# The last piece of x issued as two transfers, 120 partitions and then 8, in a convolution kernel

## The chip, the cores and the metric

The kernel runs on one core of one Trainium2 chip. The metric is device microseconds of an execution, the median of several runs. A core has TensorE (matmuls; PE in the profile, PEld for its weight loads), VectorE (DVE), ScalarE (ACT), GpSimd (POOL) and SyncE (SP), each with an instruction stream of its own. The engines wait for each other on semaphores. Data comes from memory by transfers (DMAs) that an engine issues; 16 DMA engines carry them out.

## The reference

x has the shape (4, 1024, 48, 48). It is normalised over 32 groups of channels per image, and then a recurrence runs down the 48 rows and back up. Each step multiplies the row before with a 1024 x 1024 matrix, adds a bias, takes the positive part and adds the row:

```python
def _gn(v, G=32, eps=1e-05):
    g = v.reshape(B_, G, C_ // G, H_, W_)
    m = mean(g, axis=(2, 3, 4)); s = var(g, axis=(2, 3, 4))
    return ((g - m) / sqrt(s + eps)).reshape(v.shape)
def step(carry, x):                     # Wm: the middle tap of W, 1024 x 1024
    new = relu(einsum('oc,ncw->now', Wm, carry) + bb) + x
    return (new, new)
_, ys = scan(step, xs[0], xs[1:])                       # down, rows 1 to 47
down = concatenate([xs[:1], ys])
_, ys2 = scan(step, down[-1], down[:-1], reverse=True)  # up, rows 46 to 0
return x + concatenate([ys2, down[-1:]])
```

Nothing of the recurrence can begin before the mean and the variance of all of x are known.

## The kernel before

Channels are split into K = 8 blocks of P = 128 partitions. The 48 rows are split into six groups of eight rows; x lies in memory as one block of 128 x 12288 floats for each group. In the first stage SyncE loads the groups one after another, alternately into two buffers (x_ring and d_rows), and each in pieces of a few channel blocks, as LOADS (line 33) lists them. The group loaded last (index LAST = 5, which is also the group that stays in x_ring for the first rows of the recurrence) has five pieces: blocks 0-1, 2-3, 4-5, 6 and 7. The fifth piece is channel block 7: 128 partitions with 6144 bytes each, 768 KB. load_group (line 260) issues one transfer for a piece, at line 267, after waits that say that the buffer's blocks have been read by VectorE (line 264) and ScalarE (line 265). Each piece has a semaphore of its own, stat_loaded[g][n], which a transfer raises by 16 when it has landed.

The order of SyncE's work is written out by hand: groups 0 to 4, then eight tiles of the weights (line 278, t from 0 to 7), then group 5 (line 280), then the other eight tiles (line 281), 256 KB each. After that SyncE waits until the first row is normalised (line 284) and goes on to the stores and loads of the recurrence.

The statistics are shared between two engines. VectorE takes bn_stats of each image of a channel block (line 476, channel_stats), and ScalarE does the same with two accumulating activations for two blocks of a group (lines 394 and 399, block_moments); ACT_BLOCKS (line 36) gives it blocks 3 and 7 of the first groups and blocks 1 and 5 of the last. For the last group VectorE goes piece by piece (lines 505 to 509): it waits for the piece, takes its statistics, and aggregates (line 501, channel_moments) the blocks that LAST_MOMENTS (line 37) lists for that piece: none for the first, then blocks 0 and 1, 2 and 3, 4, and 6, 5 and 7 after the fifth. When all eight blocks have moments, TensorE averages them over the groups of 32 channels (line 602), VectorE makes the spread, TensorE averages again (line 605), ScalarE takes the root (line 415), and VectorE normalises the first row (lines 535 and 538). ScalarE rounds the weight tiles (line 379, w_round) in between: tiles 8 to 11 after its last statistics and before the root, tiles 12 to 15 after it. GpSimd makes the rounding remainder of each tile (line 318), ten of them before it waits for the first row.

Then the recurrence runs on TensorE, in 283 jobs of 24 matmuls each in three-term split precision (lines 627, 634 and 640), with the other engines moving and splitting the products.

Of the kernel before, what the change touches and what calls it, by code (L numbers as in the profile page):

```python
# [12 lines left out]
P = 128  # L13
# [16 lines left out]
RING = 8  # L30
GROUPS = H // RING
LAST = GROUPS - 1
LOADS = (((0, 2), (2, 4), (4, 8)),) + (((0, 4), (4, 8)),) * (LAST - 1) + (((0, 2), (2, 4), (4, 6), (6, 7), (7, 8)),)
EARLY = RING * COLS // NI * LAST
WARM = 8
ACT_BLOCKS = ((3, 7),) * LAST + ((1, 5),)
LAST_MOMENTS = ((), (0, 1), (2, 3), (4,), (6, 5, 7))
# [33 lines left out]
def second_done(i):  # L71
    return 2 * i + 2
# [7 lines left out]
def build(nc, x_groups, w_t, bias, down_rows, out_groups):  # L80
    with ExitStack() as ctx:
# [3 lines left out]
        def sem(name):  # L85
            return ctx.enter_context(nc.semaphore(name))
# [28 lines left out]
        channels = [turn[:, (1 + t) * HALF:(2 + t) * HALF].rearrange("p (k c) -> p k c", k=KB) for t in range(2)]  # L115
        bn = turn[:, 0:K * NI * LAST * BN_DIM].rearrange("p (c s) -> p c s", c=K * NI)
        bn_late = turn[:, K * NI * LAST * BN_DIM:K * NI * (LAST * BN_DIM + BN_DIM + 3)].rearrange("p (c s) -> p c s", c=K * NI)

        def act_stat(g, k):

            images = slice(k * NI, (k + 1) * NI)
            return bn[:, images, 3 * g:3 * g + 3] if g < LAST else bn_late[:, images, 3:6]

        def act_count(g, k1):

            return sum(len(ks) for ks in ACT_BLOCKS[:g]) + sum(k < k1 for k in ACT_BLOCKS[g])

        def w_place(t):

            o, n = divmod(t, K)  # L130
            return o, KB * blocks_of(o)[n // KB] + n % KB
# [11 lines left out]
        def landing(g):  # L143

            return x_ring if g % 2 == 0 or g == LAST else d_landing

        def stats_count(g, k1):

            return sum(len(p) for p in LOADS[:g]) + [b for _, b in LOADS[g]].index(k1) + 1

        def stats_free(g, k1):

            older = g - 1 if g == LAST else g - 2
            return stats_count(older, min(b for _, b in LOADS[older] if b >= k1))

        def stat_cols(ring, i):
            return ring[:, i // NI, :, i % NI * WIDTH:(i % NI + 1) * WIDTH]

        def spare(n):

            return xn[:, n, 0:RING * WIDTH].rearrange("p (r w) -> p r w", r=RING)
# [5 lines left out]
        def row_in(groups, h, k0=0, k1=K):  # L167

            return groups[h // RING].rearrange("p (k r e) -> p k r e", k=K, r=RING)[:, k0:k1, h % RING, :]

        def ring_row(h, k0=0, k1=K):
            return x_ring[:, k0:k1, h % RING, :]
# [41 lines left out]

        stat_loaded = [[sem(f"stat_loaded{g}_{n}") for n in range(len(LOADS[g]))] for g in range(GROUPS)]
        bias_loaded = sem("bias_loaded")
# [40 lines left out]
        @block.sync  # L257
        def _(sp):

            def load_group(g):  # L260
                ring = landing(g)
                for n, (k0, k1) in enumerate(LOADS[g]):
                    if g >= 2:
                        sp.wait_ge(stats_done, stats_free(g, k1))
                        sp.wait_ge(act_read, act_count(g - 1 if g == LAST else g - 2, k1))
                    there = x_groups[LAST - g].rearrange("p (k e) -> p k e", k=K)[:, k0:k1, :]
                    sp.dma_start(ring[:, k0:k1, :, :].rearrange("p k r e -> p k (r e)"), there
                                 ).then_inc(stat_loaded[g][n], 16)

            def load_weights(t):  # L270
                o, k = w_place(t)
                sp.dma_start(w_raw[t], w_t[k, :, o * HALF:(o + 1) * HALF]).then_inc(w_loaded[t], 16)

            for g in range(LAST):
                load_group(g)
            sp.wait_ge(stats_done, stats_count(LAST - 2, K))
            sp.wait_ge(act_read, act_count(LAST - 2, K))
            for t in range(W_FRONT):
                load_weights(t)
            load_group(LAST)  # L280
            for t in range(W_FRONT, W_TILES):
                load_weights(t)

            sp.wait_ge(first_row, 4)
            sp.dma_start(down_rows[0, :, :], d_ring[:, 0, :]).then_inc(d_stored[0], 16)
            sp.dma_start(ring_row(0), row_in(x_groups, RING)).then_inc(x_loaded[0], 16)

            for h in range(1, H - RING):
                sp.wait_ge(y_ready, second_done(CHUNKS * h - 1))
                sp.dma_start(down_rows[h, :, :], d_ring[:, h % RING, :]).then_inc(d_stored[h % RING], 16)  # L290
                sp.dma_start(ring_row(h), row_in(x_groups, h + RING)).then_inc(x_loaded[h % RING], 16)

            for h in reversed(range(1, H)):
                sp.wait_ge(out_ready, CHUNKS * (H - h))
                sp.dma_start(row_in(out_groups, h), ring_row(h)).then_inc(out_stored[h % RING], 16)
                if h >= RING:
                    sp.wait_ge(d_stored[h % RING], 16 * LAST)
                    sp.dma_start(d_ring[:, h % RING, :], down_rows[h - RING, :, :]).then_inc(d_loaded[h % RING], 16)
                above = h + 1
                if RING <= above < H:  # L300
                    sp.wait_ge(out_stored[above % RING], 16 * ((H - 1 - above) // RING + 1))
                    sp.dma_start(ring_row(above), row_in(x_groups, above - RING)
                                 ).then_inc(x_loaded[above % RING], 16)
            sp.wait_ge(out_ready, CHUNKS * H)
            sp.dma_start(row_in(out_groups, 0, KB, K), ring_row(0, KB, K)).then_inc(out_stored[0], 16)
            for n, (k0, k1) in enumerate(LAST_PIECES):
                sp.wait_ge(last_out, n + 1)
                sp.dma_start(row_in(out_groups, 0, k0, k1), ring_row(0, k0, k1)).then_inc(out_stored[0], 16)
            for r in range(RING):
                sp.wait_ge(out_stored[r], 16 * (GROUPS if r else GROUPS + len(LAST_PIECES)))  # L310
# [62 lines left out]
        def _(act):  # L373
# [14 lines left out]
            def block_moments(g, k):  # L388
                count = act_count(g, k + 1)
                piece = [k < b for _, b in LOADS[g]].index(True)  # L390
                neg = act_neg[:, g, ACT_BLOCKS[g].index(k), :]
                act.wait_ge(stat_loaded[g][piece], 16)
                for n in range(NI):
                    final = act.activation(spare(n), stat_cols(landing(g), k * NI + n), ACT.Identity,  # L394
                                           scale=-1.0 / (RING * WIDTH), accum_out=neg[:, n:n + 1])
                final.then_inc(act_summed, 1)
                act.wait_ge(act_summed, count)
                for n in range(NI):
                    final = act.activation(spare(n), stat_cols(landing(g), k * NI + n), ACT.Square,  # L399
                                           bias=neg[:, n:n + 1], accum_out=act_stat(g, k)[:, n, 2:3])  # L400
                final.then_inc(act_read, 1)
                act.activation(act_stat(g, k)[:, :, 1], neg, ACT.Copy, scale=-1.0).then_inc(act_means, 1)
                act.wait_ge(act_read, count)
# [56 lines left out]
        def _(dve):  # L460
# [9 lines left out]
            def channel_stats(g, k0, k1):  # L470
                ring = landing(g)
                for i in range(k0 * NI, k1 * NI):
                    if i // NI in ACT_BLOCKS[g]:
                        continue
                    out = bn[:, i, g * BN_DIM:(g + 1) * BN_DIM] if g < LAST else bn_late[:, i, 0:BN_DIM]
                    final = dve.bn_stats(out, stat_cols(ring, i))  # L476
                return final

            for g in range(LAST):
                for n, (k0, k1) in enumerate(LOADS[g]):  # L480
                    dve.wait_ge(stat_loaded[g][n], 16)
                    channel_stats(g, k0, k1).then_inc(stats_done, 1)

            dve.memset(bn_late[:, :, BN_DIM:BN_DIM + 1], float(EARLY))
# [18 lines left out]

            dve.wait_ge(early_ready, 2)
            for n, (k0, k1) in enumerate(LOADS[LAST]):
                dve.wait_ge(stat_loaded[LAST][n], 16)
                channel_stats(LAST, k0, k1).then_inc(stats_done, 1)
                dve.wait_ge(stats_done, stats_count(LAST, k1))
                channel_moments(LAST_MOMENTS[n])
# [183 lines left out]
```

## Time and profile before

| what | value |
|---|---|
| time, median of 3 runs | 1658.34 us (1658.21 to 1658.56) |
| span of the profiled execution | 1656.3 us |
| its mean granted clock of TensorE | 1.000 of full speed |
| TensorE matmul busy | 1546.1 us (93% of the span) |
| ScalarE busy | 1358.5 us (82%) |
| VectorE busy | 1141.4 us (69%) |
| GpSimd busy | 960.0 us (58%) |
| first averaging matmul of the moments | at 102.56 us |
| first matmul of the recurrence | at 107.75 us |

The span runs from the first to the last instruction of one profiled execution; the profile gives no other time for that execution, and what lies before and after the span (launch and end) is in the runs' times alone. The chain of waits is followed back from the last instruction: at each step to what released it, or to the instruction before it on its engine. In a timeline, what stands in square brackets behind a row is idle time of the engine before it, and what ended it. A transfer's time to landing runs from its issue until its semaphore is complete.

### The profile page before, as it was taken

The page shows a single profiled execution, that of the slowest core. Times are in us where ns is not written, and L with a number is a line of the kernel's source. Part 1 is how long each engine was busy: PE and PEld are TensorE (multiplying, and loading weights), DVE is VectorE, ACT ScalarE, POOL GpSimd, SP SyncE. Part 2 cuts the span into 40 slices and gives each one's busy share as a digit, 9 for nine tenths or more (in the row PEclk, how much of TensorE's full clock was granted, in tenths as well). Part 3 has the DMA queues.
Part 4 walks back from the last instruction along what each step waited for, and adds up shares of the span by engine and source line. Part 5 has one row for each costly group of instructions (what it writes and reads, how often), then busy time and mean ns, then how long its engine had stood idle before and what let it go on. Part 6 is the DMA issues. An engine that isn't in the chain of part 4 may idle for free.

```text
span 1656.3 us, 23710 instructions
## 1 busy us (share of the span) xinstructions
PE 1546.1 (93%) x6812; PEld 1277.0 (77%) x6812; DVE 1141.4 (69%) x3355; ACT 1358.5 (82%) x4265; POOL 960.0 (58%) x1096
## 2 busy tenths in 40 slices
PE   0049999999999999999999999999999999999998
PEld 0037888888888888888888888888888888888886
DVE  5786666766766667666676666766766667666676
ACT  5658888888888888888888888888888888888887
POOL 0066766767667666676675555555555555555554
PEclk9999999999999999999999999999999999999999
DMA  9952323232323232231001444444453535454211
GB/s 406 422 224 77 106 86 115 77 115 77 115 77 115 88 104 96 96 104 50 1 1 54 157 132 155 149 137 152 135 168 119 171 122 166 125 162 135 95 58 58
DMA packets 149555, 207.06 MB, mean 125 GB/s; under 512 B 4016, under 2 KB 135088, under 8 KB 147632
## 3 DMA queue, kind: packets, MB, share of 16 engines
q1 hardware_dynamic: 149280, 205.54, 37.1%
q8 instruction: 54, 0.88, 0.2%
q14 instruction: 77, 0.63, 0.1%
q10 hardware_dynamic: 144, 0.00, 0.0%
HBM read 136.32 MB, written 69.21 MB: 124 GB/s over the span
## 4 chain that ended last, share of the span: by engine, by line
PE 91%; DMA 4%; DVE 3%; ACT 1%; issue 0%; POOL 0%; SPq 0%; ACTq 0%; DVEq 0%
PE bank L640 30%; PE bank L634 30%; PE bank L627 30%; DMA x_ring<-x_groups 4%; DVE turn L476 1%; DVE turn L562 0%; ACT turn L439 0%; DVE d_rows L538 0%; DVE d_rows L535 0%; ACT turn L430 0%; DVE st_lo L542 0%; DVE d_rows L577 0%; DVE moments L501 0%; ACT xn L399 0%; DVE turn L557 0%
## 5 line engine op out<-in xcount | busy, mean ns | idle before, releaser
L627 PE MATMUL bank<-w_hi,st_hi 128*128 128x512 f32 (+1 forms) x2264 | 881.4, 389 | 0.0
L640 PE MATMUL bank<-w_hi,st_lo 128*128 128x512 f32 (+1 forms) x2264 | 880.0, 389 | 0.6 <-DVE st_lo L542 0.3
L634 PE MATMUL bank<-w_lo,st_hi 128*128 128x512 f32 (+1 forms) x2264 | 879.9, 389 | 0.0
L355 POOL TENSOR_TENSOR st_lo<-d_rows,st_hi 128x256 fp32r<-128x256 f32 x650 | 464.0, 738 | 578.0 <-ACT st_hi L448 578.0
L430 ACT ACTIVATE turn<-turn 32x128 f32<-32x128 f32 x2256 | 697.0, 309 | 65.6 <-DVE turn L557 41.6
L562 DVE STREAM_TRANSPOSE turn<-bank 32x128 f32<-32x128 f32 x2256 | 709.6, 315 | 35.5
L640 PEld LDWEIGHTS bank<-w_hi,st_lo 128*128 128x128 f32 (+1 forms) x2264 | 424.2, 187 | 90.8 <-POOL st_lo L355 1.2
L627 PEld LDWEIGHTS bank<-w_hi,st_hi 128*128 128x128 f32 (+1 forms) x2264 | 424.4, 187 | 89.3 <-ACT st_hi L448 0.4
L634 PEld LDWEIGHTS bank<-w_lo,st_hi 128*128 128x128 f32 (+1 forms) x2264 | 424.4, 187 | 89.1 <-issue 0.2
L439 ACT ACTIVATE turn<-turn,bias_sb 128x128 f32<-128x128 f32 (+1 forms) x1132 | 362.4, 391 | 41.8 <-DVE turn L562 3.5
L448 ACT ACTIVATE st_hi<-d_rows 128x256 fp32r<-128x256 f32 x650 | 237.3, 414 | 137.9 <-DVE d_rows L577 137.9
L577 DVE TENSOR_TENSOR d_rows<-turn,xn 128x256 f32<-128x256 f32 x282 | 107.8, 423 | 199.9 <-ACT turn L439 199.9
L577 DVE TENSOR_TENSOR d_rows<-turn,d_rows 128x256 f32<-128x256 f32 x281 | 106.9, 422 | 197.5 <-ACT turn L439 197.5
L349 POOL TENSOR_TENSOR x_ring<-x_ring,d_rows 128x512 f32<-128x512 f32 x143 | 184.8, 1293 | 7.2 <-DVE d_rows L577 7.2
L557 DVE STREAM_TRANSPOSE turn<-bank 128x256 f32<-128x256 f32 (+1 forms) x283 | 127.3, 450 | 48.2 <-PE bank L640 47.6
L336 POOL TENSOR_TENSOR xn<-xn,gn_rstd 128x512 f32<-128x512 f32 x141 | 150.1, 1065 | 11.1
L334 POOL TENSOR_TENSOR xn<-x_ring,gn_mean 128x512 f32<-128x512 f32 x141 | 150.4, 1066 | 0.0
L602 PE MATMUL bank<-moments,group_avg 128*128 128x32 f32 x2 | 0.6, 396 | 102.6 <-DVE moments L501 102.6
L602 PEld LDWEIGHTS bank<-moments,group_avg 128*128 128x128 f32 x2 | 0.5, 309 | 102.5 <-issue 102.5
L318 POOL TENSOR_TENSOR w_lo<-d_rows,w_hi 128x512 fp32r<-128x512 f32 x16 | 21.9, 1398 | 95.1 <-ACT w_hi L379 89.7
L476 DVE BATCH_NORM_STATS2 turn<-x_ring 128x6 f32<-128x384 f32 x96 | 45.2, 544 | 18.2 <-DMA x_ring<-x_groups 18.1
L394 ACT ACTIVATE xn<-x_ring 128x384 f32<-128x384 f32 x32 | 16.3, 511 | 24.0 <-DMA x_ring<-x_groups 24.0
(45 smaller groups left out, 125.5 us busy)
## 6 DMA issues: line engine op xcount, KB each, us to landing
x_ring<-x_groups SPq DMA_DIRECT2D x82, 768.0 KB, 7.2
out_groups<-x_ring SPq DMA_DIRECT2D x47, 768.0 KB, 5.1
down_rows<-d_rows SPq DMA_DIRECT2D x40, 768.0 KB, 3.8
d_rows<-down_rows SPq DMA_DIRECT2D x40, 768.0 KB, 6.6
x_ring<-x_groups SPq DMA_DIRECT2D x5, 3072.0 KB, 23.6
d_rows<-x_groups SPq DMA_DIRECT2D x4, 3072.0 KB, 23.9
x_ring<-x_groups SPq DMA_DIRECT2D x5, 1536.0 KB, 10.9
d_rows<-w_t SPq DMA_DIRECT2D x16, 256.0 KB, 11.9
```

Of the source, the lines that this page charges most:

```text
L334: pool.tensor_tensor(dst, x_chunk(h, c), table(gn_mean), ALU.subtract).then_inc(centred, 1)
L336: pool.tensor_tensor(dst, dst, table(gn_rstd), ALU.mult).then_inc(xn_ready, 1)
L349: pool.tensor_tensor(x_chunk(h, c), x_chunk(h, c), by_image(d_chunk(h, c)), ALU.add).then_inc(out_ready, 1)
L355: final = pool.tensor_tensor(slot(st_lo, at, b * KB, (b + 1) * KB), d_chunk(row_of(i), i % CHUNKS, b * KB, (b + 1) * KB), slot(st_hi, at, ...
L430: final = act.activation(target(j, q, u), source(blocks, q, u), ACT.Copy)
L439: final = act.activation(cols, cols, ACT.Relu, bias=bias_sb[:, k:k + 1])
L448: final = act.activation(slot(st_hi, at, b * KB, (b + 1) * KB), d_chunk(row_of(i), i % CHUNKS, b * KB, (b + 1) * KB), ACT.Copy)
L562: final = dve.transpose(target(j, q, u), source(bank[j % BANKS], q, u))
L577: dve.tensor_tensor(here, product_of(j, i), addend, ALU.add).then_inc(y_ready, 1)
L627: return pe.matmul(bank[j % BANKS][0:used(j), :], stationary(st_hi, j, k), w_cols(w_hi, o, k), start=(n == 0), stop=False)
L634: return pe.matmul(bank[j % BANKS][0:used(j), :], stationary(st_hi, j, k), w_cols(w_lo, o, k), start=False, stop=final)
L640: return pe.matmul(bank[j % BANKS][0:used(j), :], stationary(st_lo, j, k), w_cols(w_hi, o, k), start=False, stop=final)
```

## The change

The fifth piece of the last group is issued as two transfers, partitions 0 to 119 and then partitions 120 to 127. Both raise the same semaphore by 16, and VectorE waits for 32 on it. All other pieces are issued as before, and all waits for them ask for 16.

```diff
+UNEVEN = 120
...
+        def parts(g, n):
+
+            return ((0, UNEVEN), (UNEVEN, P)) if (g, n) == (LAST, len(LOADS[LAST]) - 1) else ((0, P),)
+
+        def piece_landed(g, n):
+            return 16 * len(parts(g, n))
...
                     there = x_groups[LAST - g].rearrange("p (k e) -> p k e", k=K)[:, k0:k1, :]
-                    sp.dma_start(ring[:, k0:k1, :, :].rearrange("p k r e -> p k (r e)"), there
-                                 ).then_inc(stat_loaded[g][n], 16)
+                    here = ring[:, k0:k1, :, :].rearrange("p k r e -> p k (r e)")
+                    for p0, p1 in parts(g, n):
+                        sp.dma_start(here[p0:p1], there[p0:p1]).then_inc(stat_loaded[g][n], 16)
...
             for n, (k0, k1) in enumerate(LOADS[LAST]):
-                dve.wait_ge(stat_loaded[LAST][n], 16)
+                dve.wait_ge(stat_loaded[LAST][n], piece_landed(LAST, n))
                 channel_stats(LAST, k0, k1).then_inc(stats_done, 1)
```

The same replacement of 16 by piece_landed(g, n) stands in block_moments (ScalarE) and in the loop over the first five groups (VectorE), where it gives 16.

## Rows read from the trace of the kernel before

**Rows 1.** The page's part 4: shares of the chain by engine, by line.
```profile
PE 91%; DMA 4%; DVE 3%; ACT 1%; issue 0%; POOL 0%; SPq 0%; ACTq 0%; DVEq 0%
PE bank L640 30%; PE bank L634 30%; PE bank L627 30%; DMA x_ring<-x_groups 4%; DVE turn L476 1%; DVE turn L562 0%; ACT turn L439 0%; DVE d_rows L538 0%; DVE d_rows L535 0%; ACT turn L430 0%; DVE st_lo L542 0%; DVE d_rows L577 0%; DVE moments L501 0%; ACT xn L399 0%; DVE turn L557 0%
```

**Rows 2.** Chain in order of time, 75.5 to 108 us: start, us, what.
```profile
76.06 14.21 DMA x_ring<-x_groups
...
102.56 0.62 PE bank L602 x2
...
104.57 0.30 ACT gn_std L415
...
107.73 0.43 ACT st_hi L383
```

**Rows 3.** Timeline of SyncE's issues, 82 to 119 us: start, us, what.
```profile
82.94 0.33 SPq L267 DMA_DIRECT2D x_ring<-x_groups  x1
83.36 0.39 SPq L267 DMA_DIRECT2D x_ring<-x_groups  x1
83.84 0.39 SPq L267 DMA_DIRECT2D x_ring<-x_groups  x1
84.28 0.43 SPq L272 DMA_DIRECT2D d_rows<-w_t  x1
...
91.14 1.70 SPq L272 DMA_DIRECT2D d_rows<-w_t  x1
118.01 0.33 SPq L285 DMA_DIRECT2D down_rows<-d_rows  x1
```

**Rows 4.** DMA issues, one window each: pieces 3, 4, 5, tiles 8, 15, bias.
```profile
x_ring<-x_groups SPq DMA_DIRECT2D x1, 1536.0 KB, 11.0
x_ring<-x_groups SPq DMA_DIRECT2D x1, 768.0 KB, 13.2
x_ring<-x_groups SPq DMA_DIRECT2D x1, 768.0 KB, 14.7
d_rows<-w_t SPq DMA_DIRECT2D x1, 256.0 KB, 14.9
d_rows<-w_t SPq DMA_DIRECT2D x1, 256.0 KB, 12.6
...
bias_sb<-bias ACTq DMA_DIRECT2D x1, 4.0 KB, 4.3
```

**Rows 5.** Timeline of VectorE, 90 to 103 us.
```profile
90.37 3.78 DVE L476 BATCH_NORM_STATS2 turn<-x_ring 128x6 f32<-128x384 f32 x8 [0.63 <-DMA x_ring<-x_groups]
...
97.29 1.90 DVE L476 BATCH_NORM_STATS2 turn<-x_ring 128x6 f32<-128x384 f32 x4
99.22 0.40 DVE L501 BATCH_NORM_AGGREGATE moments<-turn 128x2 f32<-128x9 f32 x4
99.54 1.90 DVE L476 BATCH_NORM_STATS2 turn<-x_ring 128x6 f32<-128x384 f32 x4
101.47 0.94 DVE L501 BATCH_NORM_AGGREGATE moments<-turn 128x2 f32<-128x9 f32 x12
```

**Rows 6.** Issues by line: ns least, median, most; all 12, last 8.
```profile
L267 SPq DMA_DIRECT2D x_ring<-x_groups x12: 327/352/438, 0.7 to 83.8; - x12
...
L272 SPq DMA_DIRECT2D d_rows<-w_t x8: 424/435/2952, 84.3 to 91.1; - x8
```

**Rows 7.** DMA queue 94.5 to 95.5 (packets, MB, share); windows, DMA share last but one.
```profile
q1 hardware_dynamic: 68, 0.41, 101.7%
...
101.50:102.00 0.50, 0.00 (x0) 0.00 (x0) 0.50 (x8) 0.37 (x1) 0.50 (x1) 1.00 0.24 90
...
102.50:103.00 0.50, 0.44 (x2) 0.47 (x2) 0.00 (x0) 0.00 (x0) 0.00 (x0) 1.00 0.08 29
```

**Rows 8.** Timeline of ScalarE, 99 to 105 us.
```profile
99.27 2.60 ACT L379 ACTIVATE w_hi<-d_rows 128x512 fp32r<-128x512 f32 x4 [0.45 <-DMA d_rows<-w_t]
104.57 0.29 ACT L415 ACTIVATE gn_std<-bank,eps 128x32 f32<-128x32 f32 x1 [2.70 <-PE bank L605]
```

**Rows 9.** Timeline of GpSimd, 96 to 118 us.
```profile
107.78 9.65 POOL L318 TENSOR_TENSOR w_lo<-d_rows,w_hi 128x512 fp32r<-128x512 f32 x6 [5.30 <-DVE d_rows L538]
```

More of the change, by code:

```diff
@@ L391, in block_moments @@
                 neg = act_neg[:, g, ACT_BLOCKS[g].index(k), :]
-                act.wait_ge(stat_loaded[g][piece], 16)
+                act.wait_ge(stat_loaded[g][piece], piece_landed(g, piece))
                 for n in range(NI):
@@ L480, in _ @@
                 for n, (k0, k1) in enumerate(LOADS[g]):
-                    dve.wait_ge(stat_loaded[g][n], 16)
+                    dve.wait_ge(stat_loaded[g][n], piece_landed(g, n))
                     channel_stats(g, k0, k1).then_inc(stats_done, 1)
```

## The prediction

> **What bounds the kernel now.** I read the chain of waits first, by engine and line [rows 1]: TensorE holds 91% of the 1656.3 us span, and the three matmul lines of the main loop take 30% each. Loading x (L267) has 4%. So the body after about 108 us is matmuls in a fixed order, and a change to one load of x can only shift the moment at which they begin: one us later there is one us at the end, and nothing in the body gives it back or enlarges it.
>
> Then I read the same chain in order of time between 75 and 108 us [rows 2]. The last DMA on it is the second of the five pieces of group 5: issued at 76.06, landed 14.21 later, at 90.28. The next transfer on this chain would have to be the piece that the change splits, and it is not there: from 90.37 on the chain is VectorE, until TensorE averages the moments at 102.56, ScalarE takes the root at 104.57, and the split of the first row follows at 107.73.
>
> The changed piece is the fifth. SyncE issues pieces 3, 4 and 5 at 82.94, 83.36 and 83.84, and weight tile 8 at 84.28 [rows 3]. The table of DMA issues gives 11.0, 13.2, 14.7 and 14.9 us from issue to landing [rows 4]. Their landings are thus 93.94, 96.56, 98.54 and 99.18 us. The last weight tile, issued at 91.14, lands 12.6 later, at 103.7.
>
> VectorE's timeline [rows 5] tells when the fifth piece is wanted. After a wait of 0.63 us ending at 90.37, no row carries a wait: statistics of one piece and aggregation of the blocks before it alternate without a gap. The fourth piece's statistics start at 97.29, an aggregation at 99.22, and the fifth piece's statistics at 99.54. The piece landed at 98.54, so it lies **1.0 us** before its use. ScalarE reads blocks 1 and 5 of this group, which are in pieces 1 and 3; it does not read the fifth.
>
> **The change, part by part.**
>
> *One more DMA issue on SyncE.* An issue from L267 takes 0.33 to 0.44 us, median 0.35; the eight weight issues behind it take 0.42 to 2.95 [rows 6]. Nearest is the issue at 83.84 itself, 0.39; the extra one may cost 0.35 to 2.95, since I have no row for a shorter partition count. It moves eight issues and nothing else: tile 8 goes from 84.28 to about 84.7, at worst 87.2, and it lands at 99.18 behind x, so more than 11 us of queue cover it. After the eight issues SyncE waits for the first row until 118.01 [rows 3]; its spare time there is 118.01 - (91.14 + 1.70) = 25 us. ScalarE's and GpSimd's queues hold no DMA in this stretch. Value taken: 0. Without that cover the cost would be the whole 0.4 us on tile 8.
>
> *The same bytes, otherwise divided.* Price of one row of 6144 B: in the stretch from 94.5 to 95.5, x alone moves, with 68 packets and 101.7% of 16 engines [rows 7]: 16 x 1.017 us / 68 = 0.239 us a packet, and 0.41 MB / 68 is 6.0 KB, one row. With 128 rows over 16 engines, 8 a piece, a piece costs 1.9 us, against 2.0 between the landings of pieces 4 and 5. In the likeliest division the 120 rows still go eight to an engine, on all engines but one, and the 8 rows add one row to some. Those engines end 0.24 us later, and with completion packets no more than one further packet later: landing at 98.8 to 99.0, 0.5 to 0.7 us before use. The excluded ends: all 120 rows on one engine is 112 rows more than its eight, 112 x 0.239 = 26.8 us; an engine relieved of its eight rows may finish 1.9 us earlier. Value taken: +0.24 on the landing, 0 on the end, because the row price and the 16 busy engines of [rows 7] are the nearest rows.
>
> One rule of the Trainium skill bears on the division. The page "DMA: Bandwidth & Descriptors", section "Why a DMA increments its semaphore by 16 and not by 1", says that a DMA issued from SyncE uses the largest number of engines, up to 16, that divides its partition count. That would make 15 engines for 120 rows and 8 for 8 rows, hence nine rows on eight engines, eight on seven, none on the last. By it the sum is +0.24 on the landing and 0 on the end, and rival A below has no place; by the trace alone the engine count is open.
>
> *A price of the second transfer itself.* The low end is weight tile 8: 256 KB that land 0.64 us behind piece 5, or 410 GB/s, the pace of x, so nothing is paid for being a transfer of its own in a filled queue. The high end is the 4 KB bias load at the start of the kernel, 4.3 us from issue to landing [rows 4]. Value: 0, since tile 8 stands directly behind the changed piece in the same queue, while the bias load went out from ScalarE as the first of x was issued, and its 4.3 us were not hidden behind transfers ahead of it.
>
> A rule that speaks against the change: the same page, section "Anatomy of one DMA — SWDGE (gpsimd) path", counts a fixed 2.0 us for each transfer, and its section "Rules for kernel authors" says that one under 64 KB pays mostly overhead; the second part has 48 KB. By it the landing would be at 100.5 and the end at 1659.3; by tile 8's row, 0. The 2.0 us are given for DMAs that GpSimd issues, and the trace has none.
>
> *A late engine.* The share of busy DMA engines falls to 0.24 between 101.5 and 102 and is still 0.08 between 102.5 and 103 [rows 7], that is 3.8 and then 1.3 of 16 engines, while the last tile lands only at 103.7. So one engine or two end about 2 us behind the rest, and a landing is that of the latest. If it is the late engine that loses its rows, the fifth piece lands up to 1.9 us earlier, at 96.6; if it gains one, 0.24 later. Either way VectorE starts on it at 99.54: it is busy with piece 4. Value: 0.
>
> *The wait on VectorE* asks for 32 in place of 16, once. Behind it in VectorE's order are four statistics (99.54, 1.90 us) and twelve aggregations (101.47, 0.94 us) [rows 5], for which TensorE waits; this is the place where lateness would bite. Its check is one instruction as before: 0.
>
> *Weights behind it.* Tile 8 already makes ScalarE wait 0.45 us before the four roundings at 99.27, which end at 101.87; ScalarE then waits 2.70 us for TensorE before the root [rows 8]. A tile 0.24 later uses up 0.24 of those 2.70. GpSimd takes its remaining six weight tiles only at 107.78, released by VectorE [rows 9]. Cost 0; past 2.70 us of lateness the root and all after it would slip, and eight rows on one engine, 8 x 0.239 = 1.9 us, don't reach that.
>
> **Sum.** 0.4 us of issue under 11 us of queue, +0.24 us of landing under 1.0 us of slack, nothing elsewhere: span 1656.3 + 0.0. The median of the runs, 1658.34, lies 2.0 us above this span, and the change touches nothing there. Forecast **1658.3 us**.
>
> **Rivals.**
>
> *A: the transfer falls on few engines (slower).* Place: the fifth piece's landing, before VectorE's statistics at 99.54. Each further row on the fullest engine costs 0.239 us; it decides once over 1.0 us is added, from five further rows on. On eight engines for both parts it is 16 rows, eight more: 1.9 - 1.0 = +0.9, 1659.2 us. On five or fewer it is at least 24 + 2 rows, 18 more: 4.3 - 1.0 = +3.3, 1661.6; on a single engine 120 more rows, 28.7 - 1.0 = +27.7, 1686 us. For it: no row shows a transfer of other than 128 partitions. Against: every stretch of x in this trace keeps all 16 engines busy. The counts by the rule quoted above leave no engine with more than nine rows.
>
> *B: the small part pays its latency in the open (slower).* If its price were the bias load's 4.3 us after the first part's landing at 98.54, VectorE would wait until 102.8: +3.3, 1661.6; a price under 1.0 shows nothing. For it: 48 KB is nearer to 4 KB in size than to the 768 KB of the piece. Against: tile 8 and the queue, issued 14 us ahead, in which the small part's start lies beside the large part's rows.
>
> *C: the late engine is relieved and it shows (faster).* Only where an execution has the fifth piece later than 99.54, against this trace; then the gain is the overshoot, at most 1.9 - 1.0 = 0.9 us: 1657.4. Against: the 1.0 us slack, and VectorE without a wait since 90.37.
>
> **How the numbers follow.** Forecast 0.86; A 0.06, of which 0.03 with over 3.3 us; B 0.03, of which 0.01 with its whole price; C 0.04; 0.01 for what none of them names. The shown runs lie within 1658.21 to 1658.56, so the range 1657.4 to 1659.4 holds the forecast with this spread, C whole and A's eight-engine case; left out are the far parts of A and B. About 0.2%, 3.3 us, is what a measurement tells from no change: slower by more has 0.03 of A and 0.01 of B, faster by more the 0.01 without a case, the rest 0.95.
>
> **What would show it.** Right: two x transfers where the fifth piece was, landing at 96.6 to 99.5; VectorE still without a wait between 90.4 and 102.4; TensorE's averaging at 102.5. The engine division shows in the busy share between 97 and 104. Wrong: a DMA named before VectorE's statistics near 99.6 (A, with a busy share that stays low until the landing; B, with one that has gone on to the weights), or the fifth piece's statistics starting before 99.5 (C).

## The result and the profile after

The changed kernel takes 1660.37 us (1660.16 to 1660.68, 21 runs) against 1658.24 us for the kernel before (1658.11 to 1658.56, 21 runs): **2.13 us slower**, ratio 1.0013, interval 1.0007 to 1.0019. That is under the 0.2% that counted as a change here, but clear of the spread of the runs, and above the forecast range of 1657.4 to 1659.4. The profiled execution has a span of 1658.5 us, 2.2 more than before.

The chain of waits of the changed kernel in order of time (start, us, what) holds a DMA where before it held VectorE alone [rows 2, 5]:

```profile
84.49 17.15 DMA x_ring<-x_groups
101.67 1.95 DVE turn L485 x4
103.64 0.95 DVE moments L510 x12
```

The DMA is the fifth piece, landed at 84.49 + 17.15 = 101.64 in place of 98.54. VectorE's timeline, in the form of [rows 5]:

```profile
90.61 3.78 DVE L485 BATCH_NORM_STATS2 turn<-x_ring 128x6 f32<-128x384 f32 x8 [0.73 <-DMA x_ring<-x_groups]
...
97.89 1.94 DVE L485 BATCH_NORM_STATS2 turn<-x_ring 128x6 f32<-128x384 f32 x4 [0.27 <-DMA x_ring<-x_groups]
99.86 0.40 DVE L510 BATCH_NORM_AGGREGATE moments<-turn 128x2 f32<-128x9 f32 x4
101.67 1.94 DVE L485 BATCH_NORM_STATS2 turn<-x_ring 128x6 f32<-128x384 f32 x4 [1.40 <-DMA x_ring<-x_groups]
103.64 0.94 DVE L510 BATCH_NORM_AGGREGATE moments<-turn 128x2 f32<-128x9 f32 x12
```

The fifth piece's statistics begin at 101.67 in place of 99.54: 2.13 us, the whole of the difference. The matmul that averages the moments moves from 102.56 to 104.73, the first matmul of the recurrence from 107.75 to 109.93, and nothing after it makes up for it.

The fourth piece, which the change leaves as it was, is late too and makes VectorE wait 0.27 us. It takes 14.4 us to landing in place of 13.2 [rows 4]:

```profile
x_ring<-x_groups SPq DMA_DIRECT2D x1, 768.0 KB, 14.4
```

In the runs below it takes 14.3 to 14.7 us wherever the fifth piece alone is split by partitions, and 13.3 or 13.4 wherever no piece of x is (the split by columns among them). So the division of the transfer behind it is what slows it.

Why the piece is late stands in the windows (stretch, length, busy us of PE, PEld, DVE, ACT and POOL with the number of instructions, TensorE's granted clock, busy share of 16 DMA engines, GB/s). The changed kernel:

```profile
94.50:98.50 4.00, 0.00 (x0) 0.00 (x0) 3.69 (x22) 3.97 (x15) 0.00 (x0) 1.00 1.03 210
98.50:101.50 3.00, 0.00 (x0) 0.00 (x0) 1.73 (x7) 0.55 (x3) 0.00 (x0) 1.00 1.02 295
94.50:95.50 1.00, 0.00 (x0) 0.00 (x0) 1.00 (x10) 1.00 (x5) 0.00 (x0) 1.00 1.06 236
```

The kernel before, in the stretch of [rows 7] that gave the price of a row:

```profile
94.50:95.50 1.00, 0.00 (x0) 0.00 (x0) 1.00 (x8) 1.00 (x6) 0.00 (x0) 1.00 1.02 406
```

Together the 16 engines are as busy as before, and they move little more than half as much. Share x 16 engines x 6144 B / rate gives what a row of 6144 B costs an engine: 1.02 x 16 x 6144 / 406 = 247 ns before, 1.06 x 16 x 6144 / 236 = **442 ns** after. Some packets of the stretch after are rows of 2048 B from the weight tiles, so the 442 ns are a price of 6144 B over both sorts; a run without the tiles, below, gives 433. So engines did not fall idle; each packet took longer.

The small packets that complete a transfer tell how many engines it used: the page of before counts 4016 packets under 512 B, the page after 4023.

```profile
DMA packets 149562, 207.06 MB, mean 125 GB/s; under 512 B 4023, under 2 KB 135095, under 8 KB 147639
```

Seven more fits 15 + 8 in place of 16: 15 engines for the 120 rows and eight for the 8 rows. The rule on the page "DMA: Bandwidth & Descriptors" of the Trainium skill, section "Why a DMA increments its semaphore by 16 and not by 1", has it so. The kernels below agree: 64 + 64 partitions have 4032 such packets (16 + 16), 126 + 2 have 4016 (14 + 2).

### The profile page after: what moved, and what is told of

It is laid out like the page before. It is cut to its first block, busy times and chain, and to the rows that moved or that the text cites. A ratio compares the mean times of both kernels' runs of the same rounds, so it can differ in the third digit from the quotient of the medians.

```text
span 1658.5 us, 23711 instructions
## 1 busy us (share of the span) xinstructions
PE 1545.9 (93%) x6812; PEld 1276.8 (77%) x6812; DVE 1141.8 (69%) x3355; ACT 1358.3 (82%) x4265; POOL 960.6 (58%) x1096
## 4 chain that ended last, share of the span: by engine, by line
PE 91%; DMA 5%; DVE 3%; ACT 1%; issue 0%; SPq 0%; POOL 0%; ACTq 0%; DVEq 0%
PE bank L649 30%; PE bank L636 30%; PE bank L643 30%; DMA x_ring<-x_groups 5%; DVE turn L485 1%; DVE turn L571 0%; ACT turn L448 0%; DVE d_rows L547 0%; DVE d_rows L544 0%; ACT turn L439 0%; DVE st_lo L551 0%; DVE d_rows L586 0%; DVE turn L566 0%; SPq L277 0%; ACT st_hi L457 0%
```

## The experiments

The theory after the result: when a transfer has other than 128 partitions, its rows are handed to the engines so that several engines at a time write to the same part of the on-chip memory, and wait for each other (theory 1, collision). Rivals: partition counts that leave engines idle or are no power of two are slow as such (theory 2); a second transfer has a price of its own (theory 3). The pace of a transfer is the time that one engine takes for one row. Times with a sign are against the kernel before.

**Two halves of 64 partitions.**

```diff
-UNEVEN = 120
+UNEVEN = 64
```

> The fifth piece as partitions 0 to 63 and then 64 to 127. Theory 1 (collision: the rows of a part are handed to the DMA engines in runs of consecutive partitions, so that two engines at a time write to the same part of the on-chip memory and each packet takes about twice its 0.24 us): packets of 6144 B at about 0.45 us while the piece moves, the piece some 1.7 us later than in the kernel before, VectorE waits about 0.7 us for it, time +0.7 us. Theory 2 (partition counts that leave engines idle or are no power of two are slow): both parts use all 16 engines, packets at 0.24 us, no wait, time as before. Theory 3 (the second transfer has a price of its own of 2 to 3 us, whatever its shape): VectorE waits 1.4 us, time +2.1 us as in the changed kernel.

Measured: 1659.88 us, +1.6 us, ratio 1.0010 (1.0001 to 1.0019). A window and a row of VectorE's timeline of this kernel:

```profile
95.00:97.00 2.00, 0.00 (x0) 0.00 (x0) 1.97 (x8) 1.97 (x9) 0.00 (x0) 1.00 1.02 221
```

```profile
100.98 1.94 DVE L485 BATCH_NORM_STATS2 turn<-x_ring 128x6 f32<-128x384 f32 x4 [0.95 <-DMA x_ring<-x_groups]
```

1.02 x 16 x 6144 / 221 = 454 ns a row. Theory 2 falls: two equal halves, powers of two, on all engines, are as slow for each row. Theory 1 had the pace right (about 0.45 us) and the time too low (+0.7).

**126 and 2 partitions** (UNEVEN = 126).

> The fifth piece as partitions 0 to 125 and then 126 to 127. Theory 1 (collision): 14 engines with nine consecutive rows each, whose starts are nine apart and so seldom meet on the same part of the memory; packets at about 0.24 us, the piece about 0.7 us later than before (ten rows on the fullest engine in place of eight), inside the 1.0 us of slack, time as before. Theory 2 (idle engines, no power of two): fewer engines than 120 uses, so at least as slow as the changed kernel, +2 us or more. Theory 3 (price of a second transfer): +2.1 us.

Measured: 1660.00 us, +1.7 us, ratio 1.0011 (1.0002 to 1.0020); VectorE waits 1.54 us, until 101.72.

```profile
95.00:97.00 2.00, 0.00 (x0) 0.00 (x0) 2.00 (x8) 1.97 (x8) 0.00 (x0) 1.00 1.04 245
```

417 ns for 6144 B, over rows of x and of the weight tiles together. Theory 1, as I had stated it (time as before), missed here; theories 2 and 3 came nearer. The series and the runs with the tiles held back, below, say by what.

**A split by columns.**

Against the changed kernel; the fifth piece is split into floats 0 to 1439 and 1440 to 1535 of each row:

```diff
-            return ((0, UNEVEN), (UNEVEN, P)) if (g, n) == (LAST, len(LOADS[LAST]) - 1) else ((0, P),)
+            e = RING * COLS
+            return ((0, e * 15 // 16), (e * 15 // 16, e)) if (g, n) == (LAST, len(LOADS[LAST]) - 1) else ((0, e),)
...
-                    for p0, p1 in parts(g, n):
-                        sp.dma_start(here[p0:p1], there[p0:p1]).then_inc(stat_loaded[g][n], 16)
+                    for e0, e1 in parts(g, n):
+                        sp.dma_start(here[:, :, e0:e1], there[:, :, e0:e1]).then_inc(stat_loaded[g][n], 16)
```

> The fifth piece as two transfers of all 128 partitions, the first 1440 floats of each row and then the last 96: the same 15 to 1 split in bytes, but no change in partitions. Theory 1 (collision) and theory 2 (partition counts): packets at the pace of before, the landing at most 0.3 us later, no wait of VectorE, time as before. Theory 3 (price of a second transfer): VectorE waits for the piece, time +2.1 us.

Measured: 1658.31 us against 1658.29, ratio 1.0000 (0.9991 to 1.0009). Window and VectorE's timeline:

```profile
95.00:97.00 2.00, 0.00 (x0) 0.00 (x0) 1.97 (x7) 1.97 (x8) 0.00 (x0) 1.00 0.99 387
```

```profile
99.48 0.40 DVE L511 BATCH_NORM_AGGREGATE moments<-turn 128x2 f32<-128x9 f32 x4
99.80 1.90 DVE L486 BATCH_NORM_STATS2 turn<-x_ring 128x6 f32<-128x384 f32 x4
```

No wait, and the rate of before (388 GB/s in the same stretch). The same bytes, the same second issue, the same wait for 32: theory 3 falls, and with it everything in the change but the partitions.

**Single transfers.** Twelve transfers in the idle stretch at the turn of the recurrence, each waited for.

```diff
+            for n, (p0, p1) in enumerate(ALONE):
+                sp.dma_start(alone[p0:p1, :], x_groups[0, p0:p1, 0:LONG]).then_inc(alone_done, 16)
+                sp.wait_ge(alone_done, 16 * (n + 1))
```

> The kernel before, with twelve transfers added one at a time in the idle stretch of the DMA queues at the turn from down to up (rows of 3840 B): loads of partitions 0-127, 0-119, 120-127, 0-63, 0-111, 0-125, 0-15, 0-127, then stores of 0-127 and 0-119, then copies from memory to memory of 128 and 120 rows. The time of the whole doesn't matter. A 3840 B packet should take 0.15 us by the pace of before. Theory 1 (collision): loads of 120 and 64 partitions take about twice as long for a packet as that of 128, 112 and 126 little more than 128, 8 and 16 partitions about four times; memory to memory 120 takes as long for a packet as 128, since nothing is written on the chip. Theory 2 (partition counts): 64, 112 and 16 at the pace of 128; 120 and 126 slow, memory to memory too. Theory 3 (price of a second transfer): all packets at the same pace.

Measured, in windows that begin in the middle of the load of 120 partitions and of the last load of 128 and reach past their ends:

```profile
766.80:769.30 2.50, 2.50 (x13) 2.07 (x12) 1.16 (x3) 1.88 (x6) 1.58 (x3) 1.00 0.36 117
785.30:787.50 2.20, 2.20 (x11) 1.83 (x10) 2.10 (x7) 1.93 (x7) 2.20 (x3) 1.00 0.38 150
```

Share x 16 x 3840 B / rate: 189 ns against 156. No factor of two, and over the whole transfers none either: 0.22 us a packet for 120 partitions, 0.20 for 64, 0.22 for 16, against 0.20 for 128, where theory 1 had twice as much for 120 and 64 and four times for 16. So theory 1 missed here. In a lone transfer of at most eight rows an engine the first packets, slow for every count, weigh heavily; I took that for the reason and repeated the experiment with more to do. (The packet times in the next expectation are such means over whole transfers.)

**Series of five.**

```diff
+            for kind, rows, times in SERIES:
+                for n in range(times):
+                    here = target[rows, n * row:(n + 1) * row]
+                    memory = x_groups[0, rows, n * row:(n + 1) * row]
...
+                    sp.dma_start(into, out).then_inc(series_done, 16)
+                landed += times
+                sp.wait_ge(series_done, 16 * landed)
```

> The kernel before, with twelve series of five transfers each ahead of the first load of x, rows of 6144 B, the five issued back to back and waited for before the next series: loads of partitions 0-127, 0-119, 0-125, 0-63, 0-111, 0-15, 0-31, 0-127 again, stores of 0-127 and 0-119, copies from memory to memory of 128 and 120 rows. The whole gets some 150 us longer, which doesn't matter. Single transfers took 0.22 us a packet for 120 partitions and 0.20 for 128 when loaded, 0.23 against 0.15 when stored; a series shows the pace without the start. Theory 1 (two engines at a time write the same part of the on-chip memory): 128 at 0.24 us a packet, loads of 120, 64 and 32 at 0.4 to 0.5, 16 at 0.8 to 0.9, 126 and 112 at 0.25 to 0.35, store of 120 above store of 128, copies of 120 like copies of 128. Theory 1b (the engines meet in the main memory they read): copies of 120 slow as well. Theory 4 (it takes transfers of both divisions side by side, the piece's and its neighbours'): loads of 120 and 64 in a series of their own keep 0.24.

The windows inside the twelve series, in the order of the expectation:

```profile
5.00:11.00 6.00, 0.00 (x0) 0.00 (x0) 0.00 (x0) 0.00 (x0) 0.00 (x0) 1.00 1.02 425
17.00:29.00 12.00, 0.00 (x0) 0.00 (x0) 0.00 (x0) 0.00 (x0) 0.00 (x0) 1.00 0.95 230
35.00:43.00 8.00, 0.00 (x0) 0.00 (x0) 0.00 (x0) 0.00 (x0) 0.00 (x0) 1.00 0.89 319
50.00:56.00 6.00, 0.00 (x0) 0.00 (x0) 0.00 (x0) 0.00 (x0) 0.00 (x0) 1.00 0.98 203
61.00:71.00 10.00, 0.00 (x0) 0.00 (x0) 0.00 (x0) 0.00 (x0) 0.00 (x0) 1.00 1.01 268
74.00:76.50 2.50, 0.00 (x0) 0.00 (x0) 0.00 (x0) 0.00 (x0) 0.00 (x0) 1.00 0.93 118
81.50:84.00 2.50, 0.00 (x0) 0.00 (x0) 0.00 (x0) 0.00 (x0) 0.00 (x0) 1.00 0.75 167
89.00:95.00 6.00, 0.00 (x0) 0.00 (x0) 0.00 (x0) 0.00 (x0) 0.00 (x0) 1.00 1.02 426
101.00:107.00 6.00, 0.00 (x0) 0.00 (x0) 0.00 (x0) 0.00 (x0) 0.00 (x0) 1.00 1.02 419
112.00:119.00 7.00, 0.00 (x0) 0.00 (x0) 0.00 (x0) 0.00 (x0) 0.00 (x0) 1.00 0.93 384
126.00:132.00 6.00, 0.00 (x0) 0.00 (x0) 0.00 (x0) 0.00 (x0) 0.00 (x0) 1.00 1.00 348
140.00:146.00 6.00, 0.00 (x0) 0.00 (x0) 0.00 (x0) 0.00 (x0) 0.00 (x0) 1.00 0.95 350
```

Worked out as above, ns an engine for a row of 6144 B:

| transfer | 128 | 120 | 126 | 64 | 112 | 16 | 32 | 128 again |
|---|---|---|---|---|---|---|---|---|
| load | 236 | 406 | 274 | 475 | 370 | 775 | 441 | 235 |
| store | 239 | 238 | | | | | | |
| memory to memory | 282 | 267 | | | | | | |

In a queue of transfers, only loads depend on the partitions. From memory to memory 120 rows cost no more than 128 do, so the reads are not it (theory 1b falls), and no neighbour of another shape is needed (theory 4 falls). The slow thing is writing into the on-chip memory. Idle engines are not it either: 126 partitions leave some idle (share 0.89, about 14 of 16) and cost less than 112, which leave none (1.01).

Of what theory 1 expected, loads of 120, 64, 32 and 126 came out; 112 came out above it, 16 a little below. It missed on the stores: it had stores of 120 above those of 128, as the single transfers had shown them, and in the series they are equal.

A rule that I had not drawn on fits these steps. The page "SBUF — State Buffer" of the Trainium skill, section "Door 1: The DMA port swizzle", says that the bandwidth of a DMA depends on how many of 16 ports its partitions reach, and that bits 2 to 4 and bit 6 of the partition number choose the port. If each engine gets a run of consecutive partitions, 64 and 32 partitions put two engines on a port, and 16 put four. From 236 ns that would be 472 and 944, an estimate by that page; measured were 475, 441 and 775. With 120, engines four apart in runs of eight share ports two by two. That section makes no difference between loads and stores; the stores of 120 partitions here (238 against 239 ns) show no such loss.

The section "The descriptor swizzle" of the page "DMA: Bandwidth & Descriptors" of the Trainium skill has a transfer of 128 partitions give each engine a port of its own, and the 236 ns, the lowest of the loads, agree. Which engine got which row no run here shows. That the price depends on the partitions of a load is shown; that engines meet on a port is a reading that fits the factors.

**The change doubled** (the fourth piece split as well).

```diff
-            return ((0, UNEVEN), (UNEVEN, P)) if (g, n) == (LAST, len(LOADS[LAST]) - 1) else ((0, P),)
+            return ((0, UNEVEN), (UNEVEN, P)) if g == LAST and n >= len(LOADS[LAST]) - 2 else ((0, P),)
```

> The change doubled: the fourth piece of the last group is split into 120 and 8 partitions as well. Theory 1: each split piece takes about 3 us longer. The fourth lands 2.5 to 3 us late and VectorE waits some 2 us for it; the fifth lands about 6 us later than in the kernel before, at 104 to 105 where VectorE wanted it at 99.5, so the time is 4.5 to 5.5 us above before, 2.5 to 3.5 above the changed kernel, with the slack of 1.0 us used only once. Theory 4 (only a boundary between the two divisions costs): the fourth and fifth have the same division, so about as much as in the changed kernel, +2 us.

Measured: 1662.32 us (1661.99 to 1663.20), +4.0 us, ratio 1.0025 (1.0015 to 1.0035). The profiled execution was the longest of these, with a span of 1661.4 us, 5.1 above before. VectorE's timeline:

```profile
100.70 1.94 DVE L485 BATCH_NORM_STATS2 turn<-x_ring 128x6 f32<-128x384 f32 x4 [2.37 <-DMA x_ring<-x_groups]
102.67 0.40 DVE L510 BATCH_NORM_AGGREGATE moments<-turn 128x2 f32<-128x9 f32 x4
104.53 1.94 DVE L485 BATCH_NORM_STATS2 turn<-x_ring 128x6 f32<-128x384 f32 x4 [1.45 <-DMA x_ring<-x_groups]
```

The waits are where theory 1 put them: 2.37 us for the fourth piece and 104.53 for the start of the fifth, in this execution. But the fourth piece landed 4.1 us later than before (100.67 against 96.56), not 2.5 to 3, and the median of the runs is half a microsecond under the range. Theory 4 (+2 us) falls again. The slack is paid only once.

**The split on a weight tile.**

```diff
+                for p0, p1 in ((0, UNEVEN), (UNEVEN, P)) if t == W_FRONT else ((0, P),):
+                    sp.dma_start(w_raw[t][p0:p1], w_t[k, p0:p1, o * HALF:(o + 1) * HALF]).then_inc(w_loaded[t], 16)
```

> The kernel before, with x as it was and the split 120 and 8 put on weight tile 8, the transfer right behind the fifth piece. The packets slow down there as well and the tile lands 0.5 to 1.5 us later; ScalarE waits that much longer before its four roundings but has 2.70 us before the root, so the time is as before (within 0.3 us). If lateness of transfers cost time without a consumer in wait, by the engines or the queue, it would be +0.5 to +1.5 us. If the fifth piece, which still moves on late engines beside the tile, is slowed by the tile's packets, its landing comes nearer to 99.5 or passes it by a few tenths.

Measured: 1658.44 us, ratio 1.0001 (0.9992 to 1.0010). ScalarE's timeline:

```profile
100.51 2.26 ACT L381 ACTIVATE w_hi<-d_rows 128x512 fp32r<-128x512 f32 x4 [1.56 <-DMA d_rows<-w_t]
104.71 0.29 ACT L417 ACTIVATE gn_std<-bank,eps 128x32 f32<-128x32 f32 x1 [1.94 <-PE bank L607]
```

The tile makes ScalarE wait 1.56 us in place of 0.45 [rows 8], and its wait before the root shrinks to 1.94: lateness that ends inside a consumer's slack costs nothing. The fifth piece, here of 128 partitions again, was issued at 83.92 and took 15.4 us, so it landed at 99.3 in place of 98.54, just before VectorE wanted it at 99.68: a split transfer slows the whole one ahead of it.

**The tiles held back.** Three kernels, with 128, 126 + 2 and 120 + 8 partitions, in which SyncE waits for the fifth piece before it issues the tiles; its first issue of a tile thus marks the landing. (With 128 partitions the kernel is that of before, and the wait asks for 16.)

```diff
             load_group(LAST)
+            sp.wait_ge(stat_loaded[LAST][-1], 32)
```

> The kernel before, with the eight weight tiles behind x issued only when the fifth piece has landed. It is the control for the two runs beside it: the fifth piece lands at about 98.5 or somewhat earlier if the tiles behind it cost it anything; the tiles come 4 us or more later, and ScalarE's roundings may then delay the root.

> 126 and 2 partitions, the weight tiles held back until the piece has landed. In the kernel with 126 and 2 the piece landed at about 101.6, 3.1 us later than before, where its pace of packets (0.29 us by nine or ten rows) explains some 1.0. If the rest comes from the weight tiles that the engines without rows begin meanwhile, and whose writes meet those of the piece, it lands at 98.8 to 99.8 here, and VectorE hardly waits. If it comes from the piece's own division (the engine with ten rows is the late one, or the two rows meet each other), it lands at 101 to 102 as before.

> 120 and 8 partitions, the weight tiles held back until the piece has landed. The packets of the 120 rows still take 0.41 to 0.44 us and eight of them in a row 3.4 us in place of 1.9; the eight rows of the second part, on two of the memory's sixteen parts, up to 0.9 more. If the tiles have no share in the delay the piece lands at 101 to 101.7 as in the changed kernel; if they have, at 100 to 101.

SyncE's timeline of the three, in that order:

```profile
98.43 2.23 SPq L272 DMA_DIRECT2D d_rows<-w_t  x5
```

```profile
100.20 0.36 SPq L281 DMA_DIRECT2D d_rows<-w_t  x1
```

```profile
100.40 0.36 SPq L281 DMA_DIRECT2D d_rows<-w_t  x1
```

With 128 partitions the tiles hardly slowed the piece: it lands at 98.54 with them and at 98.43 without. With 120 + 8, 1.9 of the 3.1 us of delay are the piece's own (100.40 - 98.54), and 1.2 (101.64 - 100.40) come from the tiles; engines that have no more rows of x can begin those while others still write the piece. The queue between 95.5 and 96.5 (packets, MB, busy share), first with 120 + 8, then with 126 + 2:

```profile
q1 hardware_dynamic: 33, 0.20, 89.3%
q1 hardware_dynamic: 51, 0.31, 85.9%
```

There are no tile rows in these: 0.893 x 16 / 33 = 0.433 us a row with 120, and 0.859 x 16 / 51 = 0.270 with 126, the pace of its series. With the tiles beside it, 6144 B had cost 0.417 in the kernel with 126 + 2, and the piece landed 1.5 us later (101.7). Which of the two sorts of packets slowed the figure does not tell, but that is what theory 1 left out with 126: a transfer is slowed not only by its own division, but by a neighbour of another one too.

The landing at 100.2 is still later than the 98.8 to 99.8 that I expected. In the run with 128 partitions the busy share falls from 0.21 to 0.06, and the piece is complete at 98.43:

```profile
96.00:97.00 1.00, 0.00 (x0) 0.00 (x0) 0.97 (x6) 0.97 (x5) 0.00 (x0) 1.00 0.21 86
97.00:98.00 1.00, 0.00 (x0) 0.00 (x0) 1.00 (x8) 1.00 (x4) 0.00 (x0) 1.00 0.06 25
```

One engine or two are some 2 us behind, as the prediction had it. Whether that late engine is one of those with ten rows, which would make up the rest, was not tried. (The times of these three, 1659.26, 1661.24 and 1661.18 us in single runs for 128, 120 and 126, include ScalarE's roundings, which come after the late tiles and delay the root.)

## Why the prediction was wrong, point by point

The step that failed is "*The same bytes, otherwise divided*": its price of a row, 0.239 us, was read in a stretch where all transfers had 128 partitions, and taken over to transfers of 120 and 8. In the changed kernel 6144 B cost 0.442 us, with the tiles held back a row cost 0.433, in a series of 120 partitions 0.406. Nine rows at 0.433 are 3.9 us, in place of 1.9 for eight at 0.239; the held run has the piece 1.9 us late. A term that the sum put at nothing makes the rest: the tiles behind the piece delayed it by 1.2 us more. Where +0.24 us was forecast for the landing, +3.1 came.

- *What bounds the kernel, the slack and the translation into time* were right: the piece lay 1.0 us before its use, so 3.1 us of lateness became 2.1, and 2.13 were measured; one us at the start was one us at the end.
- *One more issue*, *the wait for 32* and *the price of the second transfer* cost nothing, as the split by columns shows, which has all three (1658.31 against 1658.29 us). The fixed 2.0 us weighed there would have put the end at 1659.3; the columns say 0. That this sum came nearer to the result than mine is chance.
- *The division* was as expected, 15 and 8 completions, from which nine rows at most on an engine follow. What I did not ask is where the rows of an engine go. I treated an engine's time for a row as its own; the series show that it depends on which partitions are loaded together.
- *A late engine* is there (the run with 128 partitions and the tiles held back); splitting the piece did not make it land earlier.
- *Weights behind it*: tile 8 came later than the 0.24 us that I gave it. ScalarE's timeline of the changed kernel, beside [rows 8]:

```profile
102.19 2.54 ACT L388 ACTIVATE w_hi<-d_rows 128x512 fp32r<-128x512 f32 x4 [3.14 <-DMA d_rows<-w_t]
106.74 0.29 ACT L424 ACTIVATE gn_std<-bank,eps 128x32 f32<-128x32 f32 x1 [2.01 <-PE bank L614]
```

The wait grew to 3.14 us, and 2.01 were left before a root that had itself moved; so this cost nothing. But I had counted the tiles only as what is delayed, and they delay as well (1.2 us).
- *The rivals.* A had the place, the slack of 1.0 us and the shape of the result (a DMA named before VectorE's statistics, 1.40 us of wait), with the wrong mechanism: not more rows on an engine but more time for each. Its sign, a busy share that stays low until the landing, did not show: the share stayed at 1.02 to 1.06. By the signs that I gave, a DMA named and the engines gone on, the result looked like B; the split by columns, which has the second small transfer and no wait, rules B out. C did not occur.
- *The range.* I knew that no row showed a transfer of other than 128 partitions, gave 26.8 us later and 1.9 us earlier as the excluded ends, and let the range reach only to one case in between. A price that no row shows and that stands on the path after 1.0 us should have kept more of the upper side.

## What to carry to other kernels

Load into on-chip memory with all 128 partitions in one transfer, and split it by columns where it must be split: that was free, and a split by partitions cost 1.7 to 1.8 times as much for 6144 B in this kernel (417 to 454 ns against 247), even in equal halves that use every engine. A busy share of 1.0 says that the DMA engines are occupied, not that they move data at their pace; read the rate beside it. Where a piece's slack (here 1.0 us) is shorter than the time that its own rows take (1.9), a change of its shape is a change on the path until a run has shown its pace.

## What the runs showed of the hardware

- In a queue of five, loads of 16, 32, 64, 112, 120 and 126 partitions cost 775, 441, 475, 370, 406 and 274 ns an engine for a row of 6144 B, 128 partitions 236. Stores of 120 partitions (238) and copies from memory to memory (267) showed none of it.
- A transfer slows the one of another division beside it. A piece of 128 partitions took 14.3 to 14.7 us to landing with a piece split by partitions behind it, against 13.2 to 13.4. The piece of 126 + 2 landed at 101.7 with tiles of 128 partitions directly behind it and at 100.2 without.
- A lone transfer of 120 partitions and 3840 B rows hardly showed the effect (189 against 156 ns in its second half); it took a queue of them.
